# Two-pick chunks, picks made ahead of the loop, and three buffers for A's rows in an edge convolution on one core

## The reference

```
x_i = h[dst];  x_j = h[src]
feat = concat([x_i, x_j - x_i])
m = relu(feat @ W1 + b1) @ W2 + b2
out = segment_max(m, dst);  nodes without edges get 0
return x + out
```

## Time and profile before

| | |
|---|---|
| time before | 3875.31 us median of 3 runs (3875.07 to 3875.72) |
| the profiled execution | 3876.15 us, of which its span is 3874.4 us |
| busy: PE, DVE, POOL, ACT | 3151 us (81%), 2600 us (67%), 2912 us (75%), 958 us (25%) |
| PE's granted clock, mean | 0.92 of 2.4 GHz |
| gathers by POOL / picks | 2717 / 309 |

### The profile page before, as it was taken

The page is one execution under the profiler, slowest core; times in us unless marked ns, Lnnn a source line. Parts: engine busy times, 40 slices in busy tenths (PEclk is TensorE's granted clock), DMA queues, the critical chain, the costliest instruction groups (busy, mean ns, idle before and its releaser), DMA issues.

```text
span 3874.4 us, 84326 instructions
## 1 busy us (share of the span) xinstructions
PE 3151.3 (81%) x19441; PEld 1710.9 (44%) x19751; DVE 2600.0 (67%) x7920; ACT 957.9 (25%) x3840; POOL 2912.3 (75%) x3040
## 2 busy tenths in 40 slices
PE   3200069999999999999999999999999999999930
PEld 2100035555555555555555555555555555555520
DVE  5110058777777777777777777777777777777831
ACT  4420012222222222222222222222222222222200
POOL 6777777777777777777777777777777777777766
PEclk8555589999999999999999999999999999999965
DMA  9995033333333333333333333333333333333332
GB/s 365 364 413 233 27 79 96 91 96 90 93 94 90 94 94 90 93 94 90 94 94 90 93 93 90 93 94 90 90 96 90 92 95 90 90 94 92 99 92 50
DMA packets 249669, 444.44 MB, mean 115 GB/s; under 512 B 100932, under 2 KB 105913, under 8 KB 238547
## 3 DMA queue, kind: packets, MB, share of 16 engines
q1 hardware_dynamic: 91956, 221.18, 17.7%
q0 software_dynamic: 98480, 104.31, 12.9%
q10 hardware_dynamic: 58729, 113.53, 8.1%
HBM read 221.01 MB, written 217.71 MB: 113 GB/s over the span
## 4 chain that ended last, share of the span: by engine, by line
SPq 44%; issue 15%; DMA 12%; POOL 12%; DVE 9%; PE 7%; DVEq 0%; ACT 0%; POOLq 0%; ACTq 0%
SPq L337 33%; POOL rows L462 9%; SPq L389 9%; DMA a_edges<-rows 8%; PE ps_g L773 6%; DMA a_fill<-a_edges 4%; DVE state L1027 3%; DVE a_fill L998 3%; POOL a_rows L518 2%; DVE dst_all L1056 2%; SPq L411 1%; DVE rows L1065 1%; PE ps_m L794 1%; SPq L368 1%; DVE rows L1015 1%
## 5 line engine op out<-in xcount | busy, mean ns | idle before, releaser
L462 POOL DMA_INDIRECT rows<-b_table,src_idx x2717 | 2605.3, 959 | 829.4 <-issue 826.1
L773 PE MATMUL ps_g<-shared,dst_all 128*128 128x512 bf16 x11123 | 2508.1, 380 | 16.7 <-issue 0.5
L773 PEld LDWEIGHTS ps_g<-shared,dst_all 128*128 128x128 bf16 x11433 | 1107.9, 98 | 1211.7 <-issue 8.9
L998 DVE SCALAR_TENSOR_TENSOR a_fill<-a_fill,keep 128x64 f32<-128x64 f32 x3125 | 875.0, 280 | 792.5 <-DMA a_fill<-a_edges 769.6
L1027 DVE SCALAR_TENSOR_TENSOR state<-state,keep,ps_m 128x64 f32<-128x64 f32 x3125 | 859.2, 275 | 96.2 <-PE ps_m L794 73.2
L622 ACT ACTIVATE dst_all<-ident_h,key_octet 128x128 f16<-128x128 f16 x309 | 123.6, 400 | 2146.8 <-DVE state L1027 2146.1
L632 ACT ACTIVATE dst_all<-ps_g,dst_all 128x64 f32<-128x64 f32 x2472 | 541.0, 344 | 0.0
L794 PE MATMUL ps_m<-w_diag,zt 64*128 64x64 f32 x6250 | 419.6, 278 | 105.1 <-ACT zt L655 99.1
L794 PEld LDWEIGHTS ps_m<-w_diag,zt 64*128 64x128 f32 x6250 | 376.1, 188 | 251.6 <-ACT zt L655 224.4
L783 PE MATMUL ps_t<-ident,rows 128*128 128x128 f32 x1563 | 224.0, 274 | 244.1 <-DVE rows L1015 244.0
L783 PEld LDWEIGHTS ps_t<-ident,rows 128*128 128x128 f32 x1563 | 191.4, 141 | 304.3 <-DVE rows L1015 244.5
(11 more groups left out here) (123 smaller groups left out, 469.9 us busy)
## 6 DMA issues: line engine op xcount, KB each, us to landing
rows<-b_table SPq DMA_DIRECT2D x7296, 0.2 KB
a_edges<-rows SPq DMA_DIRECT2D x80, 1250.0 KB, 14.9
a_fill<-a_edges SPq DMA_DIRECT2D x312, 320.0 KB
states<-state ACTq DMA_DIRECT2D x312, 320.0 KB
rows<-b_table ACTq DMA_DIRECT2D x5376, 0.2 KB
rows<-b_table,src_idx POOLq DMA_INDIRECT x2717, 2.4
a_fill<-b_table ACTq DMA_DIRECT2D x12, 256.0 KB, 8.4
shared<-in_x_dram SPq DMA_DIRECT2D x5, 560.0 KB
```

The source lines that it names most:

```text
L462: nc.gpsimd.indirect_dma_start(out=rows[:, c % RING, t * C:(t + 1) * C], out_offset=None, in_=b_table, in_offset=at(src_idx[:, q % SRC_RIN ...
L773: last = nc.tensor.matmul(ps_g[:, half, :], key_is[:, half, g, :], table[:, g, t, :], start=(g, t) == (0, 0), stop=g == PAGES - 1)
L998: nc.vector.scalar_tensor_tensor(here, before, flag(c, 0, t), here, ALU.mult, ALU.add).then_inc(fill_step, 1)
```

## The change

- **Picks ahead of the loop.** Chunks 0 to 10 get two picked tiles each (22 picks). They are made before the loop, in a pipeline of their own: ACT spreads pick k and masks pick k-2, PE turns pick k and picks k-1, DVE matches pick k and chooses k-2. The loop makes picks from chunk 11 on.
- **Double chunks.** From chunk 40 on, every 12th chunk (40, 52, ... 304, 23 of them) has a second picked tile. Its spread and mask follow the first one's on ACT, its 37 matmuls follow the first pick's on PE at the end of the step, its match follows on DVE and its choose comes two tiles later.
- **Rings.** `key_is` has three slots (it had two), `masked` two (it had one); `ps_g` and the turned keys keep two.
- **A's rows.** AE_RING goes from 2 to 3, and SP's load of chunk c waits for the first fill of chunk c-2.
- **Early tiles.** EARLY goes from 3 to 2 (chunks 19 and 20); chunk 18 gathers that tile. The helped tile is the one before the picked ones.

```diff
-    AE_RING = 2
+    AE_RING = 3
-    FIRST_PICK = PICK_AHEAD
+    PICKED_FIRST = 11
+    PICKS_MOST = 2
+    TWICE_FROM, TWICE_EVERY = 40, 12
     def picks_in(c):
-        return FIRST_PICK <= c < CHUNKS
+        if c >= CHUNKS:
+            return 0
+        if c < PICKED_FIRST:
+            return PICKS_MOST
+        return 2 if c >= TWICE_FROM and (c - TWICE_FROM) % TWICE_EVERY == 0 else 1
+    MASK_LAG = 2
+    def loop_picks(c):
+        return picks_of(c) if c >= PICKED_FIRST else []
+    KEY_RING = 3
-    EARLY = 3
+    EARLY = 2
     def gathered_tiles(c):
-        return CHUNK - 1 - helped(c) if picks_in(c) else CHUNK
+        return CHUNK - picks_in(c) - helped(c)
...
-                if c >= 1:
-                    sp.wait_ge(fill_step, (c - 1) * CHUNK + 1)
+                if c >= AE_RING - 1:
+                    sp.wait_ge(fill_step, (c - AE_RING + 1) * CHUNK + 1)
...
-            def mask(c):
+            def mask(c, n, i):
                 act.wait_ge(picked, n + 1 + FREE)
                 act.wait_ge(octets_marked, c // BATCHED + 1)
-                act.wait_ge(chosen, n + FREE)
+                act.wait_ge(chosen, n - 1 + FREE)
...
-            for c in range(-KEYS_AHEAD, 0):
-                if picks_in(c + KEYS_AHEAD):
-                    spread_keys(c + KEYS_AHEAD)
+            for k in range(len(FIRST_PICKS) + MASK_LAG):
+                if k < len(FIRST_PICKS):
+                    spread_key(*FIRST_PICKS[k])
+                if k >= MASK_LAG:
+                    mask(*FIRST_PICKS[k - MASK_LAG])
...
-                if picks_in(c + PICK_AHEAD):
-                    pick(c + PICK_AHEAD, range(PAGES_FIRST))
+                for n, i in loop_picks(c + PICK_AHEAD)[:1]:
+                    pick(n, range(PAGES_FIRST))
...
-                if picks_in(c + KEYS_AHEAD):
-                    turn_keys(c + KEYS_AHEAD)
-                if picks_in(c + PICK_AHEAD):
-                    pick(c + PICK_AHEAD, range(PAGES_FIRST, PAGES))
+                for n, i in loop_picks(c + KEYS_AHEAD):
+                    turn_key(n)
+                for n, i in loop_picks(c + PICK_AHEAD):
+                    pick(n, range(PAGES_FIRST if i == 0 else 0, PAGES))
...
+            for k in range(len(FIRST_PICKS) + 1):
+                if k < len(FIRST_PICKS):
+                    turn_key(FIRST_PICKS[k][1])
+                if k >= 1:
+                    pick(FIRST_PICKS[k - 1][1], range(PAGES))
...
                 dve.wait_ge(keys_turned, n + 1 + FREE)
-                dve.wait_ge(picked, n - 1 + FREE)
+                dve.wait_ge(picked, max(n - KEY_RING + 1, 0) + FREE)
...
-                    if t == CHUNK - 2 and picks_in(c + CHOOSE_AHEAD):
-                        choose(c + CHOOSE_AHEAD)
+                    for n, i in loop_picks(c + CHOOSE_AHEAD):
+                        if t == CHUNK - 2 + i * LEAD:
+                            choose(c + CHOOSE_AHEAD, n, i)
```

More of the change, by code:

```diff
@@ L65, in edge_conv, with picks_of, picked_tile, helped_tile @@
     PREFIX = 17
-    FIRST_PICK = PICK_AHEAD
+    PICKED_FIRST = 11
+    PICKS_MOST = 2
+    TWICE_FROM, TWICE_EVERY = 40, 12
     def picks_in(c):
-        return FIRST_PICK <= c < CHUNKS
-    def pick_number(c):
-        return c - FIRST_PICK
-    def picks_below(c):
-        return max(0, min(c, CHUNKS) - FIRST_PICK)
-    HELP_EVERY, HELP_SEMS = 3, 8
+        if c >= CHUNKS:
[3 more added lines that the diff above has]
+        return 2 if c >= TWICE_FROM and (c - TWICE_FROM) % TWICE_EVERY == 0 else 1
+    def picks_below(c):
+        return sum(picks_in(d) for d in range(c))
+    def picks_of(c):
+        return [(picks_below(c) + i, i) for i in range(picks_in(c))]
+    FIRST_PICKS = [(c, picks_below(c) + i, i) for c in range(PICKED_FIRST) for i in range(picks_in(c))]
+    MASK_LAG = 2
+    def loop_picks(c):
+        return picks_of(c) if c >= PICKED_FIRST else []
+    def picked_tile(i):
+        return CHUNK - 1 - i
+    def helped_tile(c):
+        return CHUNK - 1 - picks_in(c)
+    KEY_RING = 3
+    HELP_EVERY, HELP_SEMS = 3, 6
     HELP_FROM, HELP_AHEAD = 24, 9
-    EARLY = 3
+    EARLY = 2
     SP_ROWS, ACT_ROWS = 24, (20, 20, 16)
@@ L113, in edge_conv @@
     PAGES_FIRST = PAGES // 2 + 1
+    assert PICKED_FIRST <= BATCHED
     with ExitStack() as ctx:
@@ L622, in spread_keys @@
                 nc.scalar.activation(key_diag[:, n % 2, :], ident_h[:, :], ACT.Copy,
-                                     scale=key_octet[:, q % 2, 0, j:j + 1]).then_inc(keys_spread, 1)
-            def mask(c):
-                n = pick_number(c)
+                                     scale=key_octet[:, q % 2, 0, j, i:i + 1]).then_inc(keys_spread, 1)
+            def mask(c, n, i):
                 act.wait_ge(picked, n + 1 + FREE)
                 act.wait_ge(octets_marked, c // BATCHED + 1)
-                act.wait_ge(chosen, n + FREE)
+                act.wait_ge(chosen, n - 1 + FREE)
                 for o in range(OCTET):
-                    last = nc.scalar.activation(masked[:, o, :], ps_g[:, n % 2, o * C:(o + 1) * C], ACT.Copy,
-                                                scale=octet_is[:, c % MARKS, o:o + 1])
+                    last = nc.scalar.activation(masked[:, n % 2, o, :], ps_g[:, n % 2, o * C:(o + 1) * C], ACT.Copy,
+                                                scale=octet_is[:, c % MARKS, i, o:o + 1])
                 last.then_inc(octet_masked, 1)
@@ L658, in step @@
                     last.then_inc(relu_done, 1)
-                if picks_in(c + CHOOSE_AHEAD):
-                    mask(c + CHOOSE_AHEAD)
+                for n, i in loop_picks(c + CHOOSE_AHEAD):
+                    mask(c + CHOOSE_AHEAD, n, i)
                 part = (c - HELP_FROM) % HELP_EVERY
@@ L762, in turn_keys, with pick @@
                 nc.tensor.matmul(ps_k[n % 2], ones_h[:, :], key_diag[:, n % 2, :], start=True, stop=True).then_inc(keys_turned, 1)
-            def pick(c, pages):
-                n = pick_number(c)
+            def pick(n, pages):
                 half = n % 2
@@ L772, in pick @@
                     for t in range(PARTS if g < PAGES - 1 else 1):
-                        last = nc.tensor.matmul(ps_g[:, half, :], key_is[:, half, g, :], table[:, g, t, :],
+                        last = nc.tensor.matmul(ps_g[:, half, :], key_is[:, n % KEY_RING, g, :], table[:, g, t, :],
                                                 start=(g, t) == (0, 0), stop=g == PAGES - 1)
@@ L991, in fill @@
                 if t == 0:
-                    before = a_fill[:, 1 - slot, W - C:W]
+                    before = a_fill[:, (slot - 1) % AE_RING, W - C:W]
                 else:
@@ L1059, in match_keys, with choose @@
                     page_keys[:, :].rearrange("p (g o) -> p g o", o=1).to_broadcast((P, PAGES, P)),
                     ALU.is_equal).then_inc(keys_matched, 1)
-            def choose(c):
-                dve.wait_ge(octet_masked, pick_number(c) + 1 + FREE)
-                nc.vector.tensor_reduce(rows[:, c % RING, W - C:W], masked[:, :, :].rearrange("p o c -> p c o"),
+            def choose(c, n, i):
+                dve.wait_ge(octet_masked, n + 1 + FREE)
+                t = picked_tile(i)
+                nc.vector.tensor_reduce(rows[:, c % RING, t * C:(t + 1) * C], masked[:, n % 2, :, :].rearrange("p o c -> p c o"),
@@ L1066, in choose @@
                                         AX_X, ALU.add).then_inc(chosen, 1)
             split_keys(0)
-            for c in range(MATCH_AHEAD):
-                if picks_in(c):
-                    match_keys(c)
+            for k in range(len(FIRST_PICKS) + MASK_LAG):
+                if k < len(FIRST_PICKS):
+                    match_key(FIRST_PICKS[k][1])
+                if k >= MASK_LAG:
+                    choose(*FIRST_PICKS[k - MASK_LAG])
             LEAD = 2
@@ L1091, in _ @@
                     split_keys((c + SPLIT_AHEAD) // BATCHED)
-                if picks_in(c + MATCH_AHEAD):
-                    match_keys(c + MATCH_AHEAD)
+                for n, i in loop_picks(c + MATCH_AHEAD):
+                    match_key(n)
                 if helped_late(c + SHIFT_AHEAD) and help_number(c + SHIFT_AHEAD) >= EARLY + 2:
```

60 lines of the change are left out of this document (27 added, 33 removed).

## The result

The changed kernel takes 3965.2 us (median of 4 runs, 3962.9 to 3966.9) against 3875.2 us: 1.0232 times the time before, 95% interval 1.0214 to 1.0250. It is 90 us slower. That is the forecast's side and inside the range, but 31 us under the likeliest figure, 3996, and 3 us from the rival in which the wait is there and the clock holds (3968). In the profiled execution (3966.9 us, span 3965.1) the lines of the code stand 20 to 22 further down: L484 is the gather, L793 the pick's matmuls, L803 the transposes, L814 the messages, L652 the mask (into `blocks`), L1020 and L1049 the fill and the maximum, L433 SP's A load, L359 its row DMAs.

What follows compares the result with a forecast made beforehand. The prediction took SP's own issue time to pace the loop, with PE close behind at 0.41 us of slack a step. Its terms, -27 - 18 - 110 + 191 + 60 + 28 - 3, gave +121 us: 3996 us, range 3935 to 4022.

Steps and rivals of the forecast that it cites:

- the rival in which the wait is there and the clock holds: Steps behind double chunks: PE waits at `ps_g` but its clock doesn't fall; 3968 us, chance 0.22.
- start of the loop: Ahead of the loop: the scatters set the start, with the early picks done before them; -27 us (bounds -20 and -29).
- steps 0 to 7: First eight steps: they hold no pick any more and take 7.69 us instead of 9.96; -18 us (-10 and -25).
- SP's pace to PE's, steps 37 to 301: Loop: SP catches up during double chunks, so PE sets all steps at 9.96 us; -110 us (-90 if SP holds some).
- 23 second picks: Double chunks: 37 matmuls and a second turn, 8.3 us each, all on PE; +191 us (bounds +184, +196).
- 23 waits at `ps_g`: Step behind each double chunk: PE waits 2.6 us for ACT's mask, which stands behind the relu; +60 us.
- the clock after them: Behind the new waits: PE's clock falls after three of four, 1.64 us each; +28 us (bounds 0 and +38).
- all else: End of the loop: the loop comes later than the gathers, so their 3.6 us of waits go; -3 us.
- The gathers' case: End: PE's slack holds the second picks and POOL's gathers set the end, 45.5 us earlier; 3830 us, chance 0.05.
- No wait: At `ps_g`: the mask comes in time, so no wait and no fall of the clock; 3908 us, chance 0.09.
- Late early picks: Ahead of the loop: PE stays at 1.2 GHz, the 22 picks end at 635, start moves +130; 4153 us, chance 0.04.
- Three buffers were no help: A's rows: three buffers don't shorten the loop, since SP's queue is late, not the ring; in the sum, no chance given.

Runs made afterwards that it cites:

- The first experiment: The changed kernel without the 23 second picks in the loop, all other parts kept: 3871.5 us, 0.9991 times the kernel before.
- the early mask: The changed kernel with ACT masking a double chunk's first pick at the end of its step before, not after the next relu: 3895.1 us, 1.0053 times the kernel before.

## Why the prediction was right, and where it was off

The sum, term by term; the measured ones come from the starts of PE's transposes in the two traces.

| term | predicted | measured | from |
|---|---|---|---|
| start of the loop | -27 | -31.6 | 481.46 for 513.05 |
| steps 0 to 7 | -18 | -25.7 | 56.1 us for 81.8 |
| SP's pace to PE's, steps 37 to 301 | -110 | -110.9 | 264 steps at 9.955 for 2739.0 |
| 23 second picks | +191 | +183.7 | 17.94 - 9.955 |
| 23 waits at `ps_g` | +60 | +60.6 | 12.59 - 9.955 |
| the clock after them | +28 | +11.6 | 7 steps of 23, 1.45 to 1.69 each |
| all else | -3 | +3.0 | the remainder |
| span | +121 | +90.7 | 3965.1 - 3874.4 |

**The bound.** That PE had 0.41 us of slack in a step and would be the next bound was right: the chain went from SP to PE, and every step from 9 to 306 but the double ones and those behind them is PE's own 9.96 us (10.01 where two keys are turned). The first experiment shows that the second picks and their waits are the whole loss. The busy share would have misled: the rule that the prediction weighed (the Trainium skill, Perfetto Trace Analysis, Identifying the Most-Contended Engine) makes PE half free, by its weight loads, which fill 267 of 500 us in the kernel with the early mask; there PE has no gap at all, and each second pick still cost its full 7.99 us. The measurement decides against the share of weight loads as a measure of PE's headroom here. That section of the Trainium skill names MFU (the matmul work done, as a share of the peak) beside it; the prediction took the weight loads alone, so the whole rule was not put to the test.

**The new wait** was right in place, cause, count and size, 2.6 us, although no row of before had it. It could be worked out because each of its parts (transposes, relu, mask) had a row; only the 0.1 us for the semaphore had none, and in the profile after PE begins 0.14 us behind the mask's eighth activation. The early mask shows that it was a matter of order in ACT's queue: ACT was idle, and the pick done, while PE waited.

**The clock** is the term that was furthest off, by 16 us, and its share was guessed and not worked out: I took a fall after three waits of four, and it came after 7 of 23. With a wait of 4.1 us it came after all 23. The mechanism was right, the share was wrong. The trace of before could have warned: it isn't so that the loop's shorter waits left the clock alone. Of PE's 25 waits over 0.9 us from step 9 on three brought a fall, of 1.42, 1.32 and 1.33 us, while waits of 1.76, 1.80 and 1.87 us brought none. Two of them, PE's timeline before:

```profile
2123.41 1.33 PE L794 MATMUL ps_m<-w_diag,zt 64*128 64x64 f32 x20 [1.32 <-ACT zt L655]
...
2124.95 5.09 PE L773 MATMUL ps_g<-shared,dst_all 128*128 128x512 bf16 x15
...
2528.67 1.33 PE L794 MATMUL ps_m<-w_diag,zt 64*128 64x64 f32 x20 [1.87 <-ACT zt L655]
...
2530.22 3.40 PE L773 MATMUL ps_g<-shared,dst_all 128*128 128x512 bf16 x15
```

So from 1.3 us up to the 2.5 us of the changed kernel the length of a wait alone doesn't decide; at 4.1 us all of them brought a fall. In the changed kernel it came after the first double chunk and then, from step 50 on, after every fourth; with two buffers after every fourth from step 50 on; and with three early tiles, where the loop is 28 us later, after every fourth too, but after others. Where in time a wait lies counts as well then; what sets the place is open.

**The start** was right in kind: the scatters set it, and they began when the zeros were stored. The zeros were done earlier than before in this execution (first scatter at 344.8 for 351.6; I had 347.9), which makes 3 of the 5 us. The gain is real, as the kernel with three early tiles shows, and would have been worth nothing by itself, as the one without second picks shows; the prediction didn't say that.

**Steps 0 to 7.** Steps 1 to 7 took 7.1 to 8.1 us each; the 7.69 us of the late steps was close. But step 0, 12.1 us before, took 4.1 us with no pick at the low clock in it; it gave 8.0 us where I had 2.3, and that is most of what this term was short. Step 8 gave 2.2 us back, with its first pick at the low clock.

**The second pick** was taken 0.3 us too dear: the step for one more matmul, 0.217 us, fits, but the second turn costs 0.05 us behind the first and not 0.28 (it lies two steps ahead of the double one, where the steps are 10.01 us).

**The rivals.** The gathers' case (3830) failed as argued: POOL is idle 147 us at the end. (It would have needed double chunks under (158 - 45)/23 = 4.9 us; the 6.9 us of the prediction only bring the loop back to the time before.) No wait: failed in the rows above, and the early mask shows what it would have given, 3895 (I had 3908). The clock held: nearest to the measured time, since only 7 falls came. Late early picks: they ended at 453.8, 7 us ahead of what I reckoned and 20 ahead of the scatters. Three buffers were no help: shown by the kernel with two. The terms' own bounds reach further than the 4020 put down for them: with SP's pace at -90 they come to some 4036. The runs came nowhere near that side.

## What to carry to other kernels

Count the slack of the next engine in one period before giving it work from the one that seems bound: here 4.9 us in twelve steps against a pick of 8. Where a producer makes two results in a row into two buffers, ask when the first will be emptied, and put its consumer's instruction where that engine is idle; the same change with the mask moved and fewer second picks is 0.8% faster than the kernel before instead of 2.3% slower. And where several engines are within a few per cent of each other, a part that speeds up one of them can show no gain until the others are relieved as well.

## What the runs showed of the hardware

PE's granted clock went from 1.00 (2.4 GHz) to 0.50 (1.2 GHz) after idle times of 2.5 us in 7 cases of 23 in the changed kernel, 6 of 23 with two buffers and 5 of 23 with three early tiles, and of 4.1 us in 23 of 23; in the kernel before it fell after 1.3 us and stayed up after 1.9 us. A fall cost 1.35 to 1.69 us of matmul time. The same wait in the same kernel, to a hundredth of a us, had either outcome, so a wait of this size can only be given a share, from runs.
